# Feed-forward half as one program by blocks of 512 tokens, with norms spread over the attention's steps and square roots on VectorE

## The reference, cut to what matters

```python
x = L0_attn_x                       # (4, 1024, 128) float32: 4096 tokens
x = x + layernorm(attn(layernorm(x)))      # 16 heads of 64, rotary q and k, causal softmax
x = x + layernorm(ffn(layernorm(x)))

def ffn(x):                         # per token, 128 wide
    h = x @ lin0_w + lin0_b
    h = silu(h @ swi1_w1 + swi1_b1) * (h @ swi1_w2 + swi1_b2)
    scores = softmax(h @ gate_w.T)                  # 8 experts
    topv, topi = top_k(scores, 4); topv /= sum(topv)
    routed = sum_e combine[:, e] * ((silu(h @ w1[e]) * (h @ w3[e])) @ w2[e])   # all 8, dense
    shared = (silu(h @ sh_w1) * (h @ sh_w3)) @ sh_w2                           # 256 wide
    h = (routed + shared) @ lin1_w + lin1_b
    return silu(h @ swi2_w1 + swi2_b1) * (h @ swi2_w2 + swi2_b2)
```

## Time and profile before

| | |
|---|---|
| median of 3 runs | 1308.08 us (1306.36 to 1308.83) |
| the profiled execution's own time | 1310.2 us |
| its span, first to last instruction | 1308.5 us |
| granted TensorE clock, mean | 0.952 of 2.4 GHz |

### The profile page before, as it was taken

The page is one execution under the profiler, slowest core; times in us unless marked ns, Lnnn a source line. Parts: engine busy times, 40 slices in busy tenths (PEclk is TensorE's granted clock), DMA queues, the critical chain, the costliest instruction groups (busy, mean ns, idle before and its releaser), DMA issues. The chain is left out here.

```text
span 1308.5 us, 34679 instructions
## 1 busy us (share of the span) xinstructions
PE 1163.0 (89%) x13520; PEld 784.9 (60%) x13520; DVE 996.1 (76%) x2157; ACT 932.6 (71%) x2057; POOL 950.4 (73%) x988
## 2 busy tenths in 40 slices
PE   4689999999999999999999999999997398898983
PEld 1236676666666676766666676766776254564651
DVE  7859787877878787877879787877843748786857
ACT  3168878778786878778787878779897565454543
POOL 3529988898888888898888889888675425554524
PEclk8559999999999999999999999999999599998997
DMA  6541515253351515253342515253200400000002
GB/s 197 125 119 44 131 37 128 67 130 85 80 130 34 130 35 130 66 130 76 89 118 46 131 35 130 66 130 81 52 3 3 135 2 1 2 1 0 0 1 65
DMA packets 50635, 96.91 MB, mean 74 GB/s; under 512 B 6704, under 2 KB 23344, under 8 KB 48432
## 3 DMA queue, kind: packets, MB, share of 16 engines
q1 hardware_dynamic: 50480, 94.81, 29.6%
HBM read 58.47 MB, written 34.60 MB: 71 GB/s over the span
## 5 line engine op out<-in xcount | busy, mean ns | idle before, releaser
L651 POOL TENSOR_TENSOR Plo<-P,Phi 128x512 f16<-128x512 f32 (+3 forms) x640 | 538.6, 868 | 141.3 <-ACT P L389 140.7
L386 ACT ACTIVATE Phi<-psS 128x512 f16<-128x512 f32 (+3 forms) x768 | 383.4, 499 | 162.5 <-PE psS L254 114.7
L389 ACT ACTIVATE P<-psS 128x512 f32<-128x512 f32 (+3 forms) x640 | 305.5, 478 | 0.0
L272 PE MATMUL psO<-V,Plo 128*128 128x65 f16 x2304 | 287.8, 194 | 0.0
L268 PE MATMUL psO<-V,Phi 128*128 128x65 f16 x2304 | 287.5, 192 | 0.0
L270 PE MATMUL psO<-V,Phi 128*128 128x64 f16 x2304 | 287.2, 192 | 0.0
L248 PE MATMUL psS<-Q,K 128*128 128x512 f16 (+3 forms) x768 | 251.4, 327 | 37.6 <-DVE Plo L509 32.0
L558 DVE TENSOR_REDUCE pmax<-psX 128x1 f32<-128x512 f32 x384 | 254.8, 684 | 25.8 <-PE psX L330 15.9
L251 PE MATMUL psS<-Q,K 65*128 65x512 f16 (+3 forms) x768 | 251.7, 328 | 0.0
L330 PE MATMUL psX<-K,Q 128*128 128x512 f16 (+5 forms) x768 | 232.1, 337 | 18.6 <-DVE pmax L558 7.0
L268 PEld LDWEIGHTS psO<-V,Phi 128*128 128x128 f16 x2304 | 218.7, 98 | 39.8 <-POOL Plo L651 4.1
(11 more groups left out here) (163 smaller groups left out, 2180.0 us busy)
## 6 DMA issues: line engine op xcount, KB each, us to landing
K<-k_way SPq DMA_DIRECT2D x48, 512.0 KB, 6.9
k_way<-HL SPq DMA_DIRECT2D x64, 256.0 KB, 3.9
q_way<-HL SPq DMA_DIRECT2D x60, 256.0 KB, 3.8
Q<-q_way SPq DMA_DIRECT2D x60, 256.0 KB, 7.1
Q<-q_way SPq DMA_DIRECT2D x15, 512.0 KB, 11.9
x<-in_x SPq DMA_DIRECT2D x4, 512.0 KB, 5.5
out<-x SPq DMA_DIRECT2D x8, 256.0 KB, 2.2
y<-in_x SPq DMA_DIRECT2D x3, 512.0 KB, 10.5
```

The costliest lines, as they stand in the source:

```text
L272: mm = nc.tensor.matmul(O, M.Plo[:, U % NP_, k * P:(k + 1) * P], V[:, HD:2 * HD + 1], start=False, stop=j == t, skip_group_check=True)
L386: nc.scalar.activation(M.Phi[:, U % NP_, 0:w], X, ACT.Exp, scale=SCALE)
L389: nc.scalar.activation(full, X, ACT.Exp, scale=SCALE).then_inc(S.exp_done, 1)
L651: nc.gpsimd.tensor_tensor(M.Plo[:, U % NP_, 0:w], M.P32[:, U % NP_, 0:w], M.Phi[:, U % NP_, 0:w], ALU.subtract).then_inc(S.lo_pool, 1)
```

## The change

- Feed-forward: the five blocks and the hardware loop become one block (`ffn_block`) whose order a planner (`ffn_plan`) writes out: 96 chunks (8 "first" gated layers, 16 shared, 64 routed, 8 "last" gated layers), one a place, with side items ("turn", "lin0", "gate", "moe", "lin1", "out") at places around them in two PSUM banks psZ. lin0 becomes three float16 products. Back products come three places after (before: two), with five buffers instead of four.
- Norms: `norm_statistics` is a generator; each `next` issues one small piece on VectorE (two bn_stats, four bn_aggr, or one of 14 tiny operations on 128x8 values), and the inverse root is made there with a bit-level first guess and four Newton rounds in place of ScalarE's square root. In the attention one piece is issued at each step: x of batches 1, 2, 3 from slot -1 step 45, slot 2 step 4, slot 3 step 4; y of batches 0, 1, 2 from slots 5, 9 and 13; `second_norm` of batches 0, 1, 2 (residual, statistics, normalising, 36 pieces each) from slot 14 steps 4 and 24 and slot 15 step 0. x for the residual is loaded again in slot 13, ahead of `mrow`. Six "zt" items in slot 15 transpose the result. Batch 3 follows in the feed-forward block, two pieces a place.
- `x_normal` of a batch stands at steps 38 to 45 of slots 0, 2 and 3.
- Slot -1: row maxima of heads 1 to 3 use all 128 rows (TensorE waits for the twin of the queries), and VectorE makes two more rotary sums.
- Weights of the feed-forward half are loaded during the attention, 13 small transfers after the first queries and six large at the end.
- Routing: `max` gives the eight sorted scores of a token, `match_replace` clears the four largest, the difference is what stays.

```diff
-                if s == -1 and u == X_STATS:
-                    variance(range(TT, NT))
+                for first, work in steady:
+                    if (s, u) >= first:
+                        next(work, None)
-                        if s == -2:
+                        if r < DVE_SUMS:                     # 6: the sums on VectorE
-                    rows = HD if s < 0 else P
+                    rows = HD if s < 0 and h == 0 else P
+X_ROOT = {1: (-1, 45), 2: (2, 4), 3: (3, 4)}
+Y_ROOT = {0: (5, 4), 1: (9, 4), 2: (13, 22)}
+Z_NORM = {0: (LAST - 1, 4), 1: (LAST - 1, 24), 2: (LAST, 0)}
+def norm_statistics(nc, M, chain, src, tiles):
+    for n, t in enumerate(tiles):
+        last = nc.vector.bn_stats(M.bn[:, t, :], src[:, n, :])
+        if n % 2:
+            got = chain.mark(last)
+            yield
+    ...
+    for _ in range(NEWTON):
+        chain.seen(got)
+        got = chain.mark(nc.vector.scalar_tensor_tensor(out=half, in0=rstd, scalar=-0.5, in1=rstd, op0=ALU.mult,
+                                                        op1=ALU.mult))
+        yield
+        chain.seen(got)
+        got = chain.mark(nc.vector.tensor_tensor(half, half, std, ALU.mult))
+        yield
+        chain.seen(got)
+        got = chain.mark(nc.vector.scalar_tensor_tensor(out=rstd, in0=half, scalar=1.5, in1=rstd, op0=ALU.add,
+                                                        op1=ALU.mult))
+        yield
+                if s + 2 == LAST:
+                    for b in range(B):
+                        sp.dma_start(x_again[b], M.x_tiles[:, b * TT:(b + 1) * TT, :]).then_inc(S.x_again[b], 16)
                 taken(sp, (s, "mt"))
                 sp.dma_start(M.Q2[HD:HD + 1, (s + 1) % 2, :, :]..., M.mrow[:])
+            due.append((len(chunks) + S2_AFTER, k))          # S2_AFTER = 6
+        at.setdefault(n - 2 if n == len(places) - 1 else n - 3, []).append(("moe", k))
+                elif kind == "moe":
+                    pe.wait_ge(S.expert_added, added_all(k))
+            for n in range(END):                              # TensorE
+                for x in at.get(n, []):
+                    side(x)
+                if chunk_at(n) is not None:
+                    hidden(chunk_at(n))
+                if chunk_at(n - BACK_LAG) is not None:
+                    back(chunk_at(n - BACK_LAG))
+    for k in range(0, N, 4):                                  # routing
+        for t in range(k, k + 4):
+            last = nc.vector.max(out=R.top[:, t, :], in_=score[:, t, 0:E])
+            ...
+            last = nc.vector.match_replace(out=R.left[:, t, :], in_to_replace=R.top[:, t, :], in_values=score[:, t, :],
+                                           imm_value=0.0)
```

More of the change, by code:

```diff
@@ L455, in _ @@
                     rope_hi(item)
-                if s == -1 and u == X_STATS:
[L457 to L463, removed]
+                for batch in range(1, B):
+                    if s == max(0, X_ROOT[batch][0]) and X_NORMAL <= u < X_NORMAL + TT:
+                        x_normal(batch * TT + u - X_NORMAL)
         @blk.vector
@@ L584, in join_max @@
                                         ALU.max).then_inc(S.row_max, 1)
[L586 to L593, removed]
-                nc.vector.tensor_scalar(M.std[:, tiles], M.mv[:, tiles, 1], EPS, None, ALU.add)
             def out_scale(Uw, n):
@@ new lines, in add @@
+            def add(n):
+                if n not in ends:
+                    return
+                _, k, c = chunks[n]
+                o = ends[n]
+                dve.wait_ge(S.expert_out, o + 1)
+                if c >= E:
+                    nc.vector.tensor_copy(R.moe[:, TB * k:TB * k + TB, :].rearrange("p t d -> p (t d)"),
+                                          R.psY[:, o % 2, :]).then_inc(S.expert_added, 1)
+                    return
+                if c == 0:
+                    for part in range(2):
+                        if k >= part * blocks // 2:
+                            for _ in routing[part]:
+                                pass
+                dve.wait_ge(S.expert_added, o)
+                for t in range(TB):
+                    acc = R.moe[:, TB * k + t, :]
+                    last = nc.vector.scalar_tensor_tensor(
+                        out=acc, in0=R.psY[:, o % 2, t * P:(t + 1) * P],
+                        scalar=M.comb[:, TB * k + t, c:c + 1], in1=acc, op0=ALU.mult, op1=ALU.add)
+                last.then_inc(S.expert_added, 1)
@@ L899, in variance, with last_norm @@
+            def last_norm():
+                x = ("out", blocks - 1)
+                z_wait(dve, x)
+                for t in range(NT - TB, NT):
+                    last = nc.vector.bn_stats(M.bn[:, t, :], out_tile(blocks - 1, t % TB))
                 then(last)
-                for t in tiles:
-                    last = nc.vector.bn_aggr(mv[i][:, t, :], bn[i][:, t, :])
+                for t in range(NT - TB, NT):
+                    last = nc.vector.bn_aggr(M.mv[:, t, :], M.bn[:, t, :])
@@ L1427, in phase_ffn @@
-        with ExitStack() as temps:
-            back_block(nc, M, S, temps, sb, ps, out)
+        R.moe = sb(stack, "moe", [P, NT, D], F32)
+        R.sg = sb(stack, "sg", [P, 2, BANK], F32)
+        R.hid32 = sb(stack, "hid32", [P, 3, BANK], F32)
+        R.hid = sb(stack, "hid", [P, HID, 2, BANK], F16)
+        R.score = sb(stack, "score", [P, NT // 2, E + TOPK], F32)
+        R.small = sb(stack, "small", [P, 4, NT // 2, 1], F32)
+        R.top = sb(stack, "top", [P, NT // 2, E], F32)
+        R.left = sb(stack, "left", [P, NT // 2, E + TOPK], F32)
@@ L1535, in build @@
         phase_attention(nc, I, M, S, sb, ps)
[L1536 removed]
+        phase_ffn(nc, M, S, sb, ps, out)
 def rotary_table():
```

1164 lines of the change are left out of this document (617 added, 547 removed).

## The result

The change makes the kernel slower: 1328.3 us (1324.38 to 1328.94, 4 runs) against 1307.83 (1306.36 to 1308.83, 4 runs), a ratio of 1.0150, 95% interval 1.0136 to 1.0163: 1.5%, and clear of noise. Forecast were 1282 us and a range of 1250 to 1308. The profiled execution has a span of 1326.8 us.

The account below looks back on a forecast made before the run. TensorE was taken to set the pace in the attention, with VectorE near, and to idle in norm chains and block boundaries of the feed-forward. Span 1308.5 + 17 (attention) - 43 (feed-forward) = 1282.5, median 1282 us; range 1250 to 1308.

Parts of the forecast that it names:

- Start, -11: Start of the attention: statistics out of TensorE's way, higher clock and smaller items save 11 us (4 to 14).
- The clock with 128 rows, -5.3: Slot -1, 60 to 84 us: 128-row products raise TensorE's clock, the stretch shrinks to VectorE's 18.7 us, saving 5.3.
- the statistics moved out of the way, -5.5: Start: VectorE no longer does 24 bn_stats at once with TensorE standing behind them, saving 5.5 us.
- rival 3: Slot -1: the clock stays at 1.2 GHz, so the 5.3 us are not saved; 1287 us, chance 0.14.
- Six norm sets, +15: Attention: six norms issued in single pieces on VectorE cost 15 us in all (0 to 44).
- I take a third, 2.5: Each norm set: of VectorE's 7.3 us beyond its free time, a third, 2.5 us, reaches TensorE.
- 1 for `x_normal`: Attention: `x_normal`'s 24 activations on ScalarE, one a step, cost 1 us (0 to 5).
- `mrow` behind the reloads, +3: Before slot 14: four reloads of x queue ahead of `mrow`, so row maxima land late, costing 3 us (0 to 7).
- Slots 14 and 15, +9: Second norms there exceed VectorE's free time, by 12 us in slot 14 and a little in slot 15: +9 (0 to 25).
- Feed-forward, -43: As one block the feed-forward half falls from 296.7 to 254 us, gaining 43 (bounds 28 and 58).
- "moe", 7 x 1.4 = 10: Routed loop: transposes of seven finished blocks each wait 1.4 us for the weighted add and a handover, 10 us.
- Rival 2: VectorE's tiny operations queue behind GpSimd and pass delays on in full, attention and routed steps: 1345 us, chance 0.12.

Follow-up runs that it names:

- experiment 8: Slot -1 row maxima with 64 rows in every product: against the changed kernel 1328.5 us (was 1328.3); against best_m 1281.6 (was 1276.4).
- Experiment 1: Changed kernel without the root's Newton rounds, 1293.4 us; or with one-input tensor_reduce in place of those operations, 1295.6; values wrong in both.
- experiment 3: Changed kernel with the norm sets of y batches 0 and 1 started at step 16 of slots 5 and 9, not step 4: 1328.8 us.
- experiment 5: Changed kernel with a finished block's transposes and lin1 one chunk later in the routed loop, except the last block: 1305.6 us.
- experiment 6: Changed kernel with only batch 0's reload of x ahead of `mrow`, the other three after the next slot's loads: 1322.1 us.
- Experiment 7: Changed kernel without the second norms' residual, statistics and root in slots 14 and 15, values wrong: 1318.8 us.
- best_m: Changed kernel with two Newton rounds, merged roots, second norms apart, later reloads of x, transposes and lin1: 1276.4 us, the fastest.

## Why the prediction was wrong

The forecast was a net of +17 - 43 = -26 us; it is +43.6 - 25.3 = +18.3. Step by step:

- **Start, -11.** -7.7 by the marks. The clock with 128 rows, -5.3: about right, 4.9 us at the first send and 5.2 to 7.5 in the time of the fastest kernel (experiment 8); the clock in the stretch rose to 0.91. So the statistics moved out of the way, -5.5, brought some 3; why no more was not looked into. By the same windows rival 3 is out, and with it the reading by TensorE's busy time alone: busy 19.9 of 21 us it stayed at 0.50. The Trainium skill ("TensorE: Matmul & The Clock Gate", Part 1) goes by that busy time alone; this case's windows disagree.
- **Six norm sets, +15: the step that failed first.** "I take a third, 2.5" of an excess of 7.3 was the mis-sized term. The six slots cost 31.4, 0.9 of it the queue in slot 13 (`mrow`'s values are ready at 929.25 and sent at 930.13), where the sum had 15 (and 1 for `x_normal`). The tiny operations were cheaper than I had (mean 0.39 to 0.58 us, not 0.7; a set 6.1 to 9.0 us of VectorE, not 12.7), but of what they added 72% reached the slot, 5.2 us a set. Experiment 1 shows the cause: with `tensor_reduce` in their place five of the slots lose 19.8 of 25.1 us. I had it that VectorE's free time would take in 5.4 of a set and spare banks two thirds of the rest; that small share came from how few waits the kernel before had the earlier trace rows, and those waits say nothing of work that isn't there yet. In slot 9 VectorE was busy 47.6 of 60 us, 12 us free, and still 4.9 of the 7.2 added passed on. That its free time did not lie at the right steps is my reading; experiment 3, which moved the operations to other steps, won nothing by it.
- **The clock after a stall: a term that the sum did not have.** I counted idle time and left the clock at 1.00 throughout the attention. In slots 2, 5 and 9 together, at clocks of 0.95, 0.97 and 0.97, TensorE is busy 7.4 us longer (3.9, 2.0 and 1.5) for the same products, of 16.6 us by which these slots grow; in slot 3 the clock stays at 1.00 and it is 0.6 of 3.7. In the feed-forward experiment 5 took 14.1 us of waits away and 22.7 of time. The earlier trace rows had it: norm_block's 0.65 and back_block's 0.81 showed that the clock falls when TensorE idles, and I used that for the head alone.
- **`mrow` behind the reloads, +3.** TensorE waited 3.3 us for it, as forecast; with the clock behind it the price was 3 to 6 (experiment 6: 3.1 by the ratios, 6.2 by the medians, slot 14 shorter by 4.4).
- **Slots 14 and 15, +9.** 20.5, of which 3 to 6 the term above. The excess of 12 us of VectorE in slot 14 was about right; that only part of it would show was not, since VectorE has no slack left there (49.1 of 51). Experiment 7 took 10.5 of the 20.5 out with the pieces themselves.
- **Feed-forward, -43.** -25.3. "moe", 7 x 1.4 = 10, is the term: I priced the add and a handover as if VectorE stood ready, but up to three operations of 0.7 to 1.1 us were ahead of it. The waits were 19.4 at these seven places (22.1 with the eighth), and experiment 5 took 22.7 us out. With 8.0 us of waits left the half takes 250 us, and 247 in best_m. My 254 had 10 of such waits in it, so the rest of the sum, 244, was near, and expert steps of 1.96 us too (1281.34 to 1283.30). Inside that rest not every term was right: the head's clock did not fall (1.00 from 1055.4 to 1072, where I had 1.2 GHz), and ScalarE loads a table six times in the half, 1.28 us each, not twice. Nor do the bounds add up: 58 is the plain sum of the terms' better ends, and the plain sum of the worse ends is a gain of 10, not 28. The 25.3 lies between 10 and 28.
- **Rival 2** had the right sign and the right cause, at 0.12. It asked for 26 us more than my 33 in its terms; the attention's alone came to 31.4 + 20.5 = 52, and the feed-forward's waits come on top. What it had wrong are the sizes: 44 for the sets where 31.4 were measured, 25 for slots 14 and 15 where 15 to 17 beside `mrow` were, and no word of the clock.
- **How long a wait is.** I read 1.75 us in the earlier trace rows as more than one GpSimd instruction, and for that copy it is so: from 255.25 to 257.00 the trace of the kernel before has the rest of a product of 384 columns (0.93 us long), one of 256 (0.68) and one of 128 (0.44), and the copy ends with the last. My step from this one-input copy to the root's operations was the mistake. The rows of slot 9 show waits of those that end with one instruction each, and the longest of all, 1.73 us in slot 13, lies beside one of 2.13. That is the rule of the Trainium skill ("SBUF — State Buffer", Who interferes with whom), for operations with two SBUF inputs, and experiment 1 shows its other half for tensor_reduce: with one input it doesn't wait at all, 184 ns at most. The copy's longer wait stays unexplained.

## What to carry to other kernels

Free time of an engine, averaged over a slot, is no cover: ask which consumer stands behind the added instruction in that engine's order, and where nothing shows it, take most of the addition as lost (here 54% or more of it in each slot), not a third of what exceeds the free time. Price every new stall of TensorE with what its clock does afterwards; here that was nothing clear in slot 3, half of the idle time again in slot 9 (1.5 on 3.3) and more than the whole in slot 2 (3.9 on 2.9). Where GpSimd is busy, count VectorE's small operations with two SBUF inputs, do not take a one-input tensor_scalar or copy for free, and make them few (one root for three batches took 12.9 us off); and do not ask for a result in the same step of the order in which it is made.

## What was not expected of the hardware

- A tensor_reduce of 128x8 from SBUF beside a busy GpSimd takes 144 to 184 ns in all 168 uses (24 of them 4 or 16 columns wide); the two-input operations in the same places take 141 to 1732, and the longest (919.47 to 921.20) ends with a GpSimd product of 2.13 us (919.05 to 921.18). One input is no safeguard by itself: the tensor_scalar of the seed takes up to 1266 ns, the copy in the earlier trace rows 1748.
- TensorE with 64-row products, busy 19.9 of 21 us, stays at 0.50 of its clock (1.2 GHz); the same row maxima with 128 rows, busy 13.2 of 21 us, are at 0.91 (experiment 8).
- Behind a wait of 3.4 us the three gated products took 1.44 us and not 0.81; with 14.1 us of such waits gone the kernel gained 22.7.
